# Seven score rounds a batch in place of eight in a one-core perceiver kernel

## The reference, cut to what matters

```
x += xattn0(layernorm(x), ctx)           # a mean over the context rows, one linear layer
x += attn0(layernorm(x))                 # self attention over 64 rows, 16 heads, with slopes
x += ffn0(layernorm(x))                  # shared part and 8 routed experts, top 2
x += xattn1(layernorm(x), ctx)           # 16 heads of 16: softmax(q k^T / 4) v over 1601 keys
x += mixer1(x)                           # causal convolution, min-GRU scan, gated feed-forward
x += ffn1(x)                             # rows and weights rounded (8 bit, ternary), gelu
```

## Time and profile before

| | us |
|---|---|
| median of 3 runs | 2135.73 |
| lowest, highest | 2132.75, 2143.18 |
| the profiled execution, its own time | 2127.42 |
| its span (first to last instruction) | 2125.6 |
| TensorE busy, share of the span | 1970.4, 93% |
| VectorE busy, share | 1327.1, 62% |
| ScalarE busy, share | 1049.7, 49% |
| GpSimd busy, share | 615.0, 29% |

### The profile page before, as it was taken

How to read it: one execution, slowest core, us unless ns; L and a number is a source line. 1 busy time by engine, 2 the same in 40 slices (tenths; PEclk the granted TensorE clock), 3 DMA queues, 4 the chain that set the end, 5 groups by cost and what they waited for, 6 DMA issues and landing times.

```text
span 2125.6 us, 72645 instructions
## 1 busy us (share of the span) xinstructions
PE 1970.4 (93%) x31796; PEld 1585.3 (75%) x31796; DVE 1327.1 (62%) x2500; ACT 1049.7 (49%) x1532; POOL 615.0 (29%) x998
## 2 busy tenths in 40 slices
PE   5789999999999999999999989999999998999987
PEld 4677777777778787787878778787777776777764
DVE  2656656856656666666666585665666666566644
ACT  3354455555465555455555544555545444434442
POOL 3222323323233232333324222332323222122201
PEclk7999999999999999999999999999999999999999
DMA  5533434343433333434333424243342321213122
GB/s 181 180 119 107 155 128 133 112 136 116 133 118 109 114 137 116 139 108 144 122 111 129 143 76 160 92 154 100 107 147 84 121 70 61 77 50 107 50 71 70
DMA packets 124471, 243.91 MB, mean 115 GB/s; under 512 B 13952, under 2 KB 44800, under 8 KB 124160
## 3 DMA queue, kind: packets, MB, share of 16 engines
q1 hardware_dynamic: 123568, 239.23, 34.1%
q10 hardware_dynamic: 592, 0.04, 0.0%
HBM read 235.94 MB, written 3.15 MB: 112 GB/s over the span
## 4 chain that ended last, share of the span: by engine, by line
PE 73%; DVE 13%; ACT 7%; issue 5%; POOL 1%; DMA 0%; SPq 0%; DVEq 0%; POOLq 0%; ACTq 0%
PE M L805 11%; PE M L812 11%; PE SC L1023 9%; PE SC L1046 8%; PE O L1067 7%; PE X L862 5%; ACT probT L1269 4%; DVE mx L1614 4%; PE SC L1039 3%; PE M L862 3%; PE X L1133 2%; PE M L906 1%; PE X L1107 1%; PE M L867 1%; PE X L841 1%
## 5 line engine op out<-in xcount | busy, mean ns | idle before, releaser
L1614 DVE TENSOR_REDUCE mx<-SC 128x4 f32<-128x1600 f32 (+1 forms) x256 | 466.6, 1823 | 138.1 <-PE SC L1023 134.7
L1269 ACT ACTIVATE probT<-SC 128x2048 f32<-128x2048 f32 (+1 forms) x256 | 398.7, 1557 | 165.9 <-PE SC L1046 165.4
L654 POOL TENSOR_TENSOR rowsT<-raw,rowsT 128x384 fp32r<-128x384 f32 (+1 forms) x256 | 280.0, 1115 | 394.9 <-ACT rowsT L1323 394.8
L812 PE MATMUL M<-wvs,rowsT 128*128 128x256 f32 x2496 | 359.4, 293 | 2.7 <-ACT kT L1208 1.4
L805 PE MATMUL M<-rowsT,wks 128*128 128x400 f32 (+1 forms) x1536 | 341.1, 362 | 11.3 <-DVE V L1415 4.4
L1208 ACT ACTIVATE kT<-M,bk 128x400 f32<-128x400 f32 (+1 forms) x256 | 151.6, 594 | 380.3 <-PE M L805 379.8
L805 PEld LDWEIGHTS M<-rowsT,wks 128*128 128x128 f32 x1536 | 269.8, 190 | 85.9 <-issue 64.0
L812 PEld LDWEIGHTS M<-wvs,rowsT 128*128 128x128 f32 x2496 | 315.9, 192 | 23.1 <-issue 3.3
L1415 DVE TENSOR_TENSOR V<-M,bv 128x256 f32<-128x256 f32 (+1 forms) x448 | 159.5, 397 | 276.6 <-PE M L812 265.9
L1023 PE MATMUL SC<-kT,bdq 32*128 32x400 f32 (+1 forms) x2048 | 245.1, 547 | 26.6 <-ACT probT L1269 22.5
L1067 PEld LDWEIGHTS O<-probT,V 128*17 128x17 f32 x13312 | 193.9, 99 | 79.9 <-issue 75.2
(11 more groups left out here) (275 smaller groups left out, 2456.5 us busy)
## 6 DMA issues: line engine op xcount, KB each, us to landing
ring<-in_ws_dram SPq DMA_DIRECT2D x428, 256.0 KB, 4.4
summed<-in_ctx_dram SPq DMA_DIRECT2D x60, 800.5 KB, 4.5
raw<-in_ctx_dram SPq DMA_DIRECT2D x64, 384.0 KB, 4.7
raw<-in_ctx_dram SPq DMA_DIRECT2D x32, 512.0 KB, 4.3
ring<-rounded_scratch SPq DMA_DIRECT2D x64, 256.0 KB, 3.9
raw<-in_ctx_dram SPq DMA_DIRECT2D x32, 321.0 KB, 4.6
out_dram<-x SPq DMA_DIRECT2D x16, 128.0 KB, 2.3
kT<-in_ctx_dram SPq DMA_DIRECT2D x2, 800.5 KB, 8.8
```

The costliest lines, as they stand in the source:

```text
L654: pool.tensor_tensor(rowsT[1][:, c, at], raw[:, c, at], rowsT[0][:, c, at], ALU.subtract).then_inc(low_ready, 1)
L812: mm = pe.matmul(bank[:, (t - 2 * a) * D:(t - 2 * a + 1) * D], rowsT[xp][:, cc, t * P:(t + 1) * P], wvs[wp][:, cc, :], start=(at == cc == ...
L1269: act.activation(probT[step % 3][0:w, :, 0:len(ts), :].rearrange("p j t q -> p j (t q)"), SC[0:w, :, 0:len(ts) * P], ACT.Exp)\
L1614: dve.tensor_reduce(mx[c][:, :, n], SC[:, :, 0:KCH[n][1]], AX.X, ALU.max).then_inc(max_used, 1)
```

## The change: what it does, and the diff

`STEPS` becomes 7. Rounds 0 to 2 are the twelve full tiles of half 0, rounds 3 to 5 those of half 1, and round 6 holds the last tile (65 keys) of both halves. The maxima are 512 columns wide in six steps; the step between them takes the last 65 keys of both halves. `LEAD` becomes 5. `kT` has four buffers and `V` two whole ones, so that VectorE adds the bias to a value piece in one instruction. Values go one a cycle, keys two at a time in steps 1, 3 and 5. The transposes `max1` and `max0` go from place A of steps 3 and 7 to place C of steps 2 and 6; `sums` goes from step 1 to step 2. The first layer starts every 12 cycles, so two pairs overlap by two cycles. The splits of rows and their loads are moved. On VectorE the first normalization of a pair (`layer0`, its second cycle) now waits for TensorE's last transpose of the pair before.

```diff
-STEPS = C * NQ
-LEAD = 6
+RB = 3
+STEPS = C * RB + 1
+LEAD = 5
-L0_START = [-22, -6, 7, 20, 33, 46] + [3 + 14 * n for n in range(4, NT - 2)]
+L0_START = [-21, -8] + [4 + 12 * n for n in range(NT - 2)]
-FIRST_CYCLE = -25
+FIRST_CYCLE = -24
+LATE = -1, 1, 2 * NT - 3
-FIRST = [[[value(4)], [value(5)], [value(6)], [value(0)], [key(0, 3)], [value(1)], [value(3)], [value(2)]],
-         [[value(4)], [value(5)], [value(6)], [value(0)], [key(0, 3)], [value(1)], [value(3)], [value(2)]]]
-SECOND = [[[key(0, 0)], [key(0, 1)], [], [key(0, 2)], [key(1, 0)], [key(1, 1)], [], [key(1, 2), key(1, 3)]],
-          [[], [key(0, 0), key(0, 1)], [], [key(0, 2)], [], [key(1, 0), key(1, 1)], [], [key(1, 2), key(1, 3)]]]
+FIRST = [[value(5)], [value(6)], [value(0)], [value(1)], [value(2)], [value(3)], [value(4)]]
+SECOND = [[key(0, 0)], [key(0, 1), key(0, 2)], [], [key(0, 3), key(1, 3)], [key(1, 0)], [key(1, 1), key(1, 2)], []]
-OWN = value(4), value(5), value(6)
+OWN = value(5), value(6)
-LOAD_AT = (1, 2, 3, 5)
+LOAD_AT = (0, 1, 1, 3)
...
 def x_fills(b, k, place):
-    if place == "B" and k == 1 and 0 < b < B:
+    if place == "B" and k == 2 and 0 < b < B:
         yield "sums", b - 1
-    if place == "A":
-        if k == 3 and 0 <= b < B:
+    if place == "C":
+        if k == 2 and 0 <= b < B:
             yield "max1", b
-        if k == 7 and 0 <= b + 1 < B:
+        if k == 6 and 0 <= b + 1 < B:
             yield "max0", b + 1
...
 def splits(b, k, late):
-    for piece, at in enumerate((-2, -1, 0, 2)):
+    for piece, at in enumerate((-2, -1, -1, 1)):
...
 def rounds_weighed(b, k):
-    return (b, (k - 2, k - 1)) if k else (b - 1, (STEPS - 2, STEPS - 1))
+    return (b, (k - 2, k - 1)) if k else (b - 1, (STEPS - 1,))
+def round_tiles(r):
+    if r == C * RB:
+        return [(c, KF) for c in range(C)]
+    return [(r // RB, t) for t in range(4 * (r % RB), 4 * (r % RB) + 4)]
+def max_columns(n):
+    if n == RB:
+        return [(c, KF * P, KR) for c in range(C)]
+    return [(n // (RB + 1), 4 * P * (n % (RB + 1)), 4 * P)]
...
-        kT = [sp.sb(f"kT{n}", [P, KP]) for n in range(3)]
-        V = [sp.sb(f"V{n}", [P, KT * H // 2, W1]) for n in range(3)]
+        kT = [sp.sb(f"kT{n}", [P, KP]) for n in range(2 * C)]
+        V = [sp.sb(f"V{n}", [P, KT * H, W1]) for n in range(2)]
...
                 def maxima(b, k):
...
-                    for j in range(4):
-                        r = slice(32 * j, 32 * j + 32)
-                        mm = pe.matmul(SC[:, j, 0:kn], bdq[mb % 2][r, c, :, :].rearrange("p e q -> p (e q)"),
-                                       keys(mb, c)[r, k0:k0 + kn], start=True, stop=True, skip_group_check=True)
+                    for at, (c, k0, kn) in enumerate(max_columns(n)):
+                        for j in range(4):
+                            r = slice(32 * j, 32 * j + 32)
+                            mm = pe.matmul(SC[:, j, at * kn:(at + 1) * kn], bdq[mb % 2][r, c, :, :].rearrange("p e q -> p (e q)"),
+                                           keys(mb, c)[r, k0:k0 + kn], start=True, stop=True, skip_group_check=True)
...
                     if kind == "value":
...
-                        for cc in range(C):
-                            ins = dve.tensor_tensor(values(n, cc)[:, 2 * a * 8:(2 * a + m) * 8, 0:HD].rearrange("p (t h) e -> p t h e", t=m),
...
+                        dve.tensor_tensor(values(n)[:, 2 * a * H:(2 * a + m) * H, 0:HD].rearrange("p (t h) e -> p t h e", t=m),
...
                 def layer0(i, q):
...
-                        if n == 0 and i and L0_TILE[i - 1] == 0:
-                            dve.wait_ge(first_kept, 1)
+                        if n == 0 and i:
+                            wait_filled(dve, (i - 1, "l0_turn3", 0, 0))
...
                 def maxima(b, k):
...
-                    dve.tensor_reduce(mx[c][:, :, n], SC[:, :, 0:KCH[n][1]], AX.X, ALU.max).then_inc(max_used, 1)
+                    if n == RB:
+                        dve.tensor_reduce(mx[:, :, :, RB].rearrange("p c j -> p j c"),
+                                          SC[:, :, 0:C * KR].rearrange("p j (c n) -> p j c n", c=C), AX.X, ALU.max).then_inc(max_used, 1)
+                    else:
+                        c, at = divmod(n, RB + 1)
+                        dve.tensor_reduce(mx[:, c, :, at], SC[:, :, :], AX.X, ALU.max).then_inc(max_used, 1)
...
-                    if (b, k) == (B, 0):
+                    if (b, k) == (B, 2):
                         hidden_max(NT - 2)
...
-    nc = bacc.Bacc("TRN2", target_bir_lowering=False, num_devices=1)
+    nc = bacc.Bacc("TRN2", target_bir_lowering=False, num_devices=1, dynamic_dma_scratch_size=1024)
```

More of the change, by code:

```diff
@@ L47 @@
 TILE = list(range(1, NT)) + [0]
[L49 removed]
+L0_PLACE = list(range(9)) + [NT - 1] + list(range(9, NT - 1))
 L0_TILE = [TILE[p] for p in L0_PLACE]
@@ L200, in query_place @@
 def query_place(b):
-    if b in (-1, 1):
+    if b in LATE:
         return (b + 1) // 2, 0
     t = b // 2 + 1
-    return (t, 5 if t == 2 else QUERIES_AT) if b > 0 and b % 2 == 0 and t < NT else (None, 0)
+    return (t, 4 if t == 2 else QUERIES_AT) if b > 0 and b % 2 == 0 and t < NT - 1 else (None, 0)
 def pieces(b, k, half):
-    for what in {"first": FIRST[b % 2][k], "second": SECOND[b % 2][k]}.get(half, ()):
+    for what in {"first": FIRST[k], "second": SECOND[k]}.get(half, ()):
         batch = b if what in OWN else b + 1
@@ L300 @@
 count_all()
-def tiles(g):
-    return range(4 * g, min(4 * g + 4, KT))
 def held(t):
@@ L728, in clear @@
                         pool.memset(mparts[c][:, :, :], 0.0)
-                    for n in range(3):
+                    for n in range(2):
                         pool.memset(V[n][:, :, HD:W1], 1.0)
```

92 lines of the change are left out of this document (48 added, 44 removed).

## The result

The changed kernel takes 2201.18 us (median of 4 runs, 2198.21 to 2203.59) against 2134.24 us beside it (2131.55 to 2143.18): ratio 1.0305, 95% interval 1.0288 to 1.0321. It is 67 us slower, and outside the range that was forecast. The profiled execution took 2198.21 us.

What follows compares the result with a forecast made beforehand. TensorE, busy 93% of the span, was taken as the bound. Terms 7-7-6+3+19-5-4+1 = +8 us on 2125.6 gave 2134 us, or 2144 against the profiled execution's median; own range 2130 to 2160, whole range 2106 to 2176.

Steps and rivals of the forecast that it cites:

- Maxima and scores on TensorE: TensorE's matmuls: regrouped maxima cost +7 us, scores save 7 us because two tiles share one round.
- Waits for the exponential: Matmuls at the score memory waiting for ScalarE's exponential: about 80 short cycles instead of 65, +3 us.
- Waits for the reduce: Scores waiting for VectorE's reduce, hand-over 3.62 us instead of 2.90: largest term, +19 us.
- steps 2 and 6 (+14): Part of the reduce term: weighing but no key piece as cover, short by 0.5 us in about 30 cycles, +14 us.
- step 0 (+12): Part of the reduce term, even batches: only two tiles weighed there, mean shortage 0.8 us in 15 batches, +12 us.
- The reduce's duration: Sign on VectorE: the reduce of 2048 columns takes 2.30 us.
- The bias in one instruction: VectorE's value bias as one 512-column instruction instead of two: 30 us less VectorE work, -4 us on the time.
- VectorE's lateness: VectorE reaches the reduce late behind second-layer work; steps 1, 3, 4, 5 absorb it, 0, 2, 6 do not: -5 us.
- A cycle less: TensorE's idle time outside score-memory waits, 0.27 us a cycle: 32 cycles less save 6 us.
- Ends: Ahead of batch 0 nothing; last but one pair's later second layer +3, one hand-over less in batch 31 -2: +1 us.
- the turn of a batch jams: Slower rival: maximum's split, copy, high and low parts crowd two cycles, ScalarE's exponential 1 us late per batch; 2170 us, chance 0.10.
- Every wait for the reduce grows: Slower rival: scores' waits in six sevenths of the remaining 90 waiting cycles grow 0.72 us each; 2171 us, chance 0.16.

Runs made afterwards that it cites:

- The runs without lumps in both kernels: Both kernels with tanh for gelu without table loads, and hidden maximum and rounding shortened: changed kernel 2150.38 us (1.0083), kernel before 2115.04 us (0.9901).
- The run with the moved pair: Kernel before with the second layer of pair 14 two cycles later, so five of its steps stand behind batch 31, not three: 2144.97 us, 1.0047.
- the same cut in both kernels: Each reduce of a maxima group read 112 columns fewer: changed kernel (400 of 512) 2175.76 us, 1.0189; kernel before (288 of 400) 2111.01 us, 0.9881.

## Why the prediction was wrong

The forecast was a sum of +8 us on the span; it came to +70.8. Of the signs that it set, the reduce's duration came out; TensorE's busy time (1993.7, forecast within 10 of 1970) and its idle time in the batches (147.7, forecast 115 to 135) did not. Step by step:

- **Maxima and scores on TensorE (+7 - 7): right to a few us.** From the start of a 512-column group to the next work it is 1.06 to 1.07 us (1.13 forecast), of the small group 0.60 (0.5), of the round of two tiles 0.68 (0.72), all read from the timeline.
- **Waits for the exponential (+3): right,** from 22.5 to 26.2 us.
- **Waits for the reduce (+19): near in size, in part by luck.** Matmuls wait 0.9 us more for the reduce, and 17.2 us for `mT` (34 times), a wait that was not there. For steps 2 and 6 (+14) the working said that the next scores wait for exactly that copy, and it is the copy that ends last. For step 0 (+12) it named the reduce, and no such growth shows on the matmuls; on the weight loads of the scores the waits for it rose from 40.0 to 52.5 us. Its count of 103 waiting cycles is a misreading: the 32 matmuls that waited stand in the same cycles as 32 of the 71 weight loads, so it was 71 cycles of 256.
- **The reduce's duration (2.30): right,** 2291 ns.
- **The bias in one instruction (-4): its saving was half of what was forecast.** VectorE's biases take 145.5 us in all for 159.5, 14 us less and not 30: the two instructions of 416 ns overlap (384 of them were busy for 144.0 us, not 160). What that did to the time was not measured.
- **VectorE's lateness (-5) failed.** The sentence was that steps 1, 3, 4 and 5 "have 2.6 us and more behind the maxima and absorb it". That cover stands against the scores' wait alone. A lump on VectorE is also ahead of the bias of the value piece, and the next piece needs that bank: the waits for the drains of `V`, on VectorE, grew from 14.3 to 22.1 us. Those for `kT`, on ScalarE, grew from 9.7 to 16.5. And the lumps had not been placed. The diff moves them by counting in cycles of seven; the working looked up the first layer in each step and never where `q` 15 and 16 fall. The runs without lumps in both kernels put what they cost more after the change at 26 us, the largest cause that was found. The 13 us of shortages from which the term starts have no working; the items beside it (1, 1 and 5) come to 7.
- **A cycle less (-6) did not show.** The idle time of a batch rose from 3.5 to 4.6 us.
- **No term for the clock.** In the batches TensorE is busy 18.9 us more, though its work by the terms above is the same or less. These us come from stretches at the lower level, by two readings. Value pieces of 12 matmuls take 1.70 us at full clock (184 of them) and 2.93 where the whole piece lies at the lower level (4). And an estimate from both traces: the matmuls at the lower level in the batches take 43 us more than the same matmuls, with the same successor, take at full clock on average; before it was 12. That difference of 31 is more than the 18.9, so the work itself did not grow.
- **Ends (+1) failed.** Behind the last scores it is +12.5 instead of +1: the last feed-forward piece, the rounding, both `up` pieces, the gelu and its tables of pair 14 now run there, one after the other. The run with the moved pair shows 10 of it in the kernel before. Ahead of the first scores it is +4.6, where 0 was forecast: with `LEAD` at 5 the first batch's transposes wait 3.2 us for GpSimd's parts of the maximum and its scores 1.9 us for the copy. No run tested that, and part of it may be the profiled execution: over the other profiles here this stretch takes 95 to 103 us with seven steps and 89 to 93 with eight.

So the step that failed is VectorE's lateness, taken as a gain of 5 us, and with it two terms that were put at nothing or nearly so: the lower clock behind the waits, and the ends. Of the gap of 65 us the lumps are 26 and the later second layer of pair 14, in the tail, about 10. The reduces are not in this list, because the same cut in both kernels left the gap at 66: six of them in a batch are longer, and there are eight before. The remaining 29 us are not assigned to a cause by any run. The new wait for `mT` (17.2 us) is among the candidates, and the credit that should have stood against it, a cycle less in each batch, was not there.

Of the rivals, "the turn of a batch jams" (2170, chance 0.10) was nearest in kind, with the wrong engine first: it is VectorE in steps 2 and 3 and, once in 12 batches, ScalarE, not the high and low parts. "Every wait for the reduce grows" (2171) had the sign and half the size, by luck: the matmuls' waits for it grew by 0.9 us, and with 71 waiting cycles for 103 it comes to about 2154. The rule named beside it (the Trainium skill, Perfetto Trace Analysis, "Optimizing Scalar/DVE Operations": instructions of an engine that isn't saturated but causes bubbles may be broken up) was not tried in its own sense, since no run broke an instruction up. What is near it points the same way: reduces that read less gained 25 us in both kernels, though VectorE is busy about 60%; but the change's longer and fewer reduces lost nothing by that (66 us with the cut, 65 without).

What is open: whether the lumps cost more because of their steps or because a round of seven has less room for them anywhere; how the 34.8 us of idle time and the 18.9 of busy time divide among the causes, since a wait and the low clock behind it come together; and whether a phase of both layers exists in which seven steps are faster. Other phases of the second layer than three steps later were not tried in the changed kernel.

## What to carry to other kernels

A change to the length of a hand-written cycle moves everything that is counted in cycles. Before the sum, write down for each long instruction outside the loop (here gelu, table loads, rounding, reciprocal) on which step it falls before and after, and what else stands there. The same layer two cycles later cost 168 us in the kernel before, where it met the sums in the one bank they share; no change of a size here cost as much. And cover behind a wait is no cover for the other waits of the same queue: ask for each late engine which buffer it should have freed.

## What the runs showed that was not expected

- A reciprocal of 256 columns takes 1.74 us on VectorE, the product behind it, over the same columns, 0.42, so one such instruction in the wrong step is as long as a reduce of 1600 columns.
- In the same 17.5 us step, 7.4 us with TensorE 56% busy were granted full clock, and the 10.1 us behind them, 99% busy, 0.66. So the price of the clock is to be looked for behind the wait, not in it.
- The clock alone does not rank two kernels. Moving the second layer in the changed kernel cost 31 us, though the mean granted clock of its four runs (0.967 to 0.975) was no lower than that of the changed kernel (0.966 to 0.967).
